# Relative attention on one NeuronCore: scores from zero-padded key copies, against scores on each head's own 32 rows

## What is computed

```python
Q, K, V = x @ W_q + b_q, x @ W_k + b_k, x @ W_v + b_v        # each to (B, 16 heads, 512, 8)
idx    = clip(k - q, -2, 2) + 2                              # 5 relative positions
scores = (einsum('bhqd,bhkd->bhqk', Q, K) + einsum('bhqd,qkd->bhqk', Q, rel_k_table[idx])) / sqrt(8)
attn   = softmax(where(causal, scores, -1e9), axis=-1)
out    = einsum('bhqk,bhkd->bhqd', attn, V) + einsum('bhqk,qkd->bhqd', attn, rel_v_table[idx])
y      = out.transpose(...).reshape(B, S, E) @ W_o + b_o
# then: x = x + y + six_windowed_layers(layernorm(x))
```

## Time and profile before

| | |
|---|---|
| time, three runs | 3923.24, 3927.83, 3929.47 us (median 3927.83) |
| profiled execution, its own time | 3928.65 us |
| its span | 3926.6 us |
| relative attention, start to last score work | about 0 to 563 us |
| windowed layers | the rest |
| PE busy over the whole span | 94% |
| DVE, ACT, POOL busy over the span | 78%, 58%, 66% |

### The profile page before, as it was taken

One profiled execution on the slowest core, in us unless ns is written; L12 is line 12 of the kernel. 1 busy time (PEld: TensorE's weight loads), 2 busy tenths in 40 slices (PEclk: granted clock), 3 DMA queues, 4 the chain that ended last, 5 costly groups with the idle time before them and its releaser, 6 DMA issues.

```text
span 3926.6 us, 163773 instructions
## 1 busy us (share of the span) xinstructions
PE 3690.6 (94%) x67712; PEld 2844.7 (72%) x67712; DVE 3058.0 (78%) x5829; ACT 2270.7 (58%) x4270; POOL 2597.4 (66%) x3029
## 2 busy tenths in 40 slices
PE   5999979999999999999999999999999999999998
PEld 3555557777767777677877678787677876777876
DVE  7666658888778888788887788887788887888876
ACT  3555546666546666456666366665466664566653
POOL 4545538787547887367887288775477873687870
PEclk8999989999999999999999999999999999999999
DMA  1000002222212222122222122222122221222220
GB/s 44 4 6 4 6 28 68 56 60 60 58 32 59 59 57 59 41 49 60 61 57 56 30 65 57 59 61 58 32 60 58 59 56 41 54 57 58 60 52 22
DMA packets 136313, 189.08 MB, mean 48 GB/s; under 512 B 38006, under 2 KB 58484, under 8 KB 135412
## 3 DMA queue, kind: packets, MB, share of 16 engines
q1 hardware_dynamic: 135540, 178.23, 17.7%
HBM read 22.67 MB, written 2.10 MB: 6 GB/s over the span
## 4 chain that ended last, share of the span: by engine, by line
PE 76%; issue 4%; DVE 2%; POOL 2%; ACT 0%; DMA 0%; POOLq 0%; SPq 0%; DVEq 0%; ACTq 0%
PE PS L1270 18%; PE PS L1417 10%; PE PS L1256 10%; PE PS L1294 8%; PE PS L1280 8%; PE PS L1258 8%; PE PS L1257 8%; PE PS L1476 2%; PE PS L1411 2%; PE PS L1454 1%; PE PS L1447 1%; POOL t L1182 1%; PE PS L1442 1%; POOL t L1187 0%; DVE m L1800 0%
## 5 line engine op out<-in xcount | busy, mean ns | idle before, releaser
L1182 POOL TENSOR_TENSOR t<-t 128x1024 f32<-128x1024 f32 x384 | 908.0, 2370 | 363.9 <-DVE t L1762 362.6
L1187 POOL TENSOR_TENSOR t<-t,rn 128x1024 f32<-128x1024 f32 x384 | 723.6, 1905 | 29.8 <-POOL rn L150 27.3
L1542 ACT ACTIVATE va<-PS 128x512 f32<-128x512 f32 x384 | 229.8, 599 | 614.4 <-PE PS L1258 611.6
L1760 DVE TENSOR_TENSOR t<-PS,rope 128x512 f32<-128x512 f32 x768 | 523.2, 681 | 26.1 <-ACT sq L1577 24.5
L1256 PE MATMUL PS<-w_hi,xh 128*128 128x512 f32 x1152 | 514.2, 446 | 22.3 <-DVE xl L1063 11.3
L1577 ACT ACTIVATE sq<-PS 128x512 f32<-128x512 f32 x768 | 454.1, 593 | 33.0 <-PE PS L1258 17.7
L1270 PE MATMUL PS<-constants,t 128*128 128x128 f32 x3072 | 443.8, 277 | 19.8 <-POOL t L1187 12.8
L1258 PE MATMUL PS<-w_lo,xh 128*128 128x512 f32 x1152 | 458.5, 398 | 0.0
L1257 PE MATMUL PS<-w_hi,xl 128*128 128x512 f32 x1152 | 457.5, 397 | 0.0
L1767 DVE TENSOR_REDUCE ss<-sq 128x16 f32<-128x1024 f32 x384 | 448.3, 1209 | 0.0
L1270 PEld LDWEIGHTS PS<-constants,t 128*128 128x128 f32 x3072 | 351.9, 141 | 68.9 <-POOL t L1187 15.9
(11 more groups left out here) (168 smaller groups left out, 7869.8 us busy)
## 6 DMA issues: line engine op xcount, KB each, us to landing
vs<-va SPq DMA_DIRECT2D x768, 130.0 KB
vs<-va SPq DMA_DIRECT2D x768, 65.0 KB
t<-in_L_ffn_Wqkv SPq DMA_DIRECT2D x18, 512.0 KB, 4.4
w_out<-in_L_ffn_Wo SPq DMA_DIRECT2D x6, 512.0 KB, 3.9
a_normed<-in_L_attn_x SPq DMA_DIRECT2D x8, 256.0 KB, 7.0
a_xo<-in_L_attn_x SPq DMA_DIRECT2D x8, 256.0 KB, 2.8
out<-total SPq DMA_DIRECT2D x8, 256.0 KB, 3.5
w_raw<-in_L_ffn_W SPq DMA_DIRECT2D x6, 341.0 KB
```

The source lines that it names most:

```text
L1182: pool.tensor_tensor(mine[:, i, :], mine[:, i, :], t2[:, i, :], ALU.add).then_inc(done, 1)
L1187: pool.tensor_tensor(h, h, bc(rn[:, H * i:H * (i + 1)], 2, HB), ALU.mult).then_inc(done, 1)
L1760: dve.tensor_tensor(o1, src, bc(rope[:, 2 * i, t, :], 1, 8), ALU.mult)
```

## The change

`kT` loses its four copies and has the same layout as `qT`. Each score product now reads only the 32 partitions of its head (`head(j, a)`), so PE works with tiles of 32 rows by 128 columns, and the two heads of a piece stand next to each other in PE's list, in different row tiles and different banks. The mask products stay as they are, over all 128 rows; the two of a piece now come first, and the scores of both heads after them.

A piece holds exactly two heads. So the fifth piece (four heads of 256 columns in a full slot) becomes two pieces that fill half of each bank: 6 pieces in place of 5. `maximum` and `weights` have one more instruction in a group, and the last two are half as long.

`join_keys` is one addition on 128 partitions. The memset of `kT` at the start of DVE's list is gone. `values(y, 0)` stands one piece later, and `values(y, 2)` moves from the end of group `y` to the place after `turned(y + 1, 0)`; the waits of `weights` on `val_mm` follow. GpSimd takes `join_queries` ahead of `keep_state` and `add_bias`, and `near_values` ahead of `add_bias`.

```diff
-        PIECES = 5
+        PIECES = 6
-        JOINS = 1 + G
+        JOINS = 2
-        kT = sb("a_kT", [P, NG, G, N], F32R)
+        kT = sb("a_kT", [P, NG, N], F32R)
...
             def join_keys(y):
                 wait_used(pool, ("proj", y, 1))
-                for r in range(G):
-                    rows = slice(32 * r, 32 * (r + 1))
-                    pool.wait_ge(joined, JOINS * y + 1 + r)
-                    pool.tensor_tensor(kT[rows, y % NG, r, 1:N], high[rows, 1, 0:N - 1].bitcast(F32), lowT[rows, 1, 0:N - 1],
-                                       ALU.add).then_inc(joined, 1)
-                pool.wait_ge(joined, JOINS * (y + 1))
+                pool.tensor_tensor(kT[:, y % NG, 1:N], high[:, 1, 0:N - 1].bitcast(F32), lowT[:, 1, 0:N - 1],
+                                   ALU.add).then_inc(joined, 1)
...
+            def head(j, a):
+                r = 2 * (j % 2) + a
+                return slice(32 * r, 32 * (r + 1))
...
             def natural(y, j):
...
-                q = lambda t: qT[:, g, P * t:P * (t + 1)]
-                k = lambda r, n: kT[:, g, r, 0:P * n]
+                blocks = (((3, 0, 4),), ((2, 0, 3), (0, 3, 1)), ((1, 0, 2),))[j // 2]
                 for a in range(2):
-                    b, r = bank(me, a), 2 * (j % 2) + a
-                    if j < 2:
-                        shut(b[:, 3 * P:4 * P], far_mask)
-                        done = score(b[:, 0:4 * P], q(3), k(r, 4))
-                    elif j < 4:
-                        shut(tiles_of(b, 2, 2), far_mask)
-                        score(b[:, 0:3 * P], q(2), k(r, 3))
-                        done = score(b[:, 3 * P:4 * P], q(0), k(r, 1))
-                    else:
-                        shut(every_second(b, 1), far_mask)
-                        for h in range(2):
-                            done = score(b[:, 2 * P * h:2 * P * (h + 1)], q(1), k(2 * a + h, 2))
+                    at, n = ((3, 1), (2, 2), (1, 1))[j // 2]
+                    shut(tiles_of(bank(me, a), at, n), far_mask)
+                for t, at, n in blocks:
+                    for a in range(2):
+                        rows = head(j, a)
+                        done = score(bank(me, a)[:, P * at:P * (at + n)], qT[rows, g, P * t:P * (t + 1)], kT[rows, g, 0:P * n])
                 done.then_inc(filled(me), 1)
...
             def turned(y, j):
...
+                    shut(tiles_of(bank(me, a), 0, (1, 2, 1)[j // 2]), far_mask_t)
+                for t, at in (((0, 0),), ((3, 0), (1, 1)), ((2, 0),))[j // 2]:
+                    for a in range(2):
+                        rows = head(j, a)
+                        done = score(bank(me, a)[:, P * at:P * (at - t) + N], kT[rows, g, P * t:P * (t + 1)],
+                                     qm[rows, y % 2, P * t:N])
...
                     turned(y, j)
+                    if j == 0 and y:
+                        values(y - 1, 2)
...
+                    if j == 3:
                         values(y, 0)
...
                 values(y, 3)
-                values(y, 2)
+            values(GROUPS - 1, 2)
...
-            dve.memset(kT[:].rearrange("p n g c -> p (n g c)").bitcast(F32), 0.0).then_inc(filled_in, 1)
             norm(0, TPS, 0)
```

More of the change, by code:

```diff
@@ L90, in constants @@
     row, query = np.arange(P)[:, None] % (2 * W), np.arange(P)[None, :]
+    c[:, C_FART:C_FART + P] = far.T
     c[:, C_SEL:C_SEL + P] = np.where(query < W, query == row, query % W + W == row)
-    c[:, C_FART:C_FART + P] = far.T
     c[0, C_NEAR:C_NEAR + H] = MASKED
@@ L365, in per_tile_head, with heads_of @@
             return h.rearrange("p t (h d) -> p t h d", h=H)
-        def of_heads(b, n):
-            return b[:, 0:G * n].rearrange("p (g c) -> p g c", g=G)
+        def heads_of(j, at, n):
+            return probs[:, 2 * (j % 2):2 * (j % 2) + 2, at:at + n]
         @block.sync
@@ L448, in _ @@
             keep_state(0)
-            pool.wait_ge(filled_in, 2 + G)
+            pool.wait_ge(filled_in, 2)
             join_queries(0)
@@ L457, in _ @@
                 s, p = divmod(y, NG)
+                if y + 3 < GROUPS:
+                    join_queries(y + 3)
                 if p == 1 and s + 1 < B:
@@ L460, in _ @@
                 if p == 3:
+                    near_values(s)
                     add_bias(s)
-                if y + 3 < GROUPS:
-                    join_queries(y + 3)
                 if p == 2 and s + 1 < B:
                     near_products(s + 1)
-                if p == 3:
-                    near_values(s)
                 if y + 3 < GROUPS:
@@ L505, in tiles_of @@
                 return b[:, P * at:P * (at + n)].rearrange("p (t c) -> p t c", t=n)
-            def every_second(b, at):
-                return b.rearrange("p (h t c) -> p h t c", h=2, t=2)[:, :, at, :]
+            def head(j, a):
+                r = 2 * (j % 2) + a
+                return slice(32 * r, 32 * (r + 1))
             def natural(y, j):
@@ L538, in turned @@
                 wait_slot(pe, me)
-                k = lambda r, t: kT[:, g, r, P * t:P * (t + 1)]
-                q = lambda t: qm[:, y % 2, P * t:N]
                 for a in range(2):
[L542 to L553, removed]
+                    shut(tiles_of(bank(me, a), 0, (1, 2, 1)[j // 2]), far_mask_t)
[4 more added lines that the diff above has]
+                                     qm[rows, y % 2, P * t:N])
                 done.then_inc(filled(me), 1)
@@ L557, in values @@
                 s, g = divmod(y, NG)
-                for j in ((0, 1), (2, 3), (4,), ())[kt]:
+                for j in ((0, 1), (2, 3), (4, 5), ())[kt]:
                     wait_used(pe, ("turn", y, j))
@@ L617, in _ @@
             pe.wait_ge(const_made, 3)
-            pe.wait_ge(filled_in, 2 + G)
+            pe.wait_ge(filled_in, 2)
             for j in range(PIECES):
@@ L680, in weights @@
                 wait_filled(act, me)
[L681 to L687, removed]
+                if y:
+                    act.wait_ge(val_mm, 4 * (y - 1) + (1, 3, 4)[j // 2])
+                at, n = ((0, 4), (4, 4), (8, 2))[j // 2]
+                act.activation(heads_of(j, P * at, P * n), bank(me)[:, :, 0:P * n], ACT.Exp, scale=SCALE_A).then_inc(used(me), 1)
             def copy_sums(y):
@@ L756, in maximum @@
                 else:
-                    target, source = maxima[:, y % 2, :, 5], bank(me).rearrange("p a (h c) -> p (a h) c", h=2)
+                    target, source = pair[:, :, 5], bank(me)[:, :, 0:2 * P]
                 dve.tensor_reduce(target, source, X, ALU.max).then_inc(used(me), 1)
@@ L841, in _ @@
             dve.wait_ge(const_in, 16)
+            dve.tensor_copy(kT[:, :, 0], rank["const"][:, C_SHUT:C_SHUT + 1].broadcast_to([P, NG])).then_inc(filled_in, 1)
             dve.wait_ge(filled_in, 2)
[L843 to L846, removed]
             dve.wait_ge(bias_made, 10)
```

## The result

The changed kernel takes 3986.77 us (median of 4 runs, 3982.11 to 3993.01), against 3925.53 for the kernel before (4 runs, 3922.84 to 3929.47): a ratio of 1.0152, 95% interval 1.0139 to 1.0165. The forecast was 3930, its range ended at 3960. The profiled execution after is the slowest of the four, 3993.01 us with a span of 3991.2.

The account below looks back on a forecast made before the run. PE was taken to bound relative attention. +17 us of PE work, -4 from relief of POOL and -11 at the start summed to +2 us on the profiled 3928.65, giving 3930 for the median, range 3900 to 3960.

Parts of the forecast that it names:

- the first reading: Relative attention after its start: PE is the bound, busy 470.30 of 492.00 us, at granted clock 0.99, the 2.4 GHz level.
- Pieces: Score pieces on PE: 512 columns 0.64 us, natural 384 and 128 0.76, turned 128 and 384 0.81, 256 columns 0.53.
- the change of shape: On PE, each switch between full-row mask products and 32-row score products costs 0.09 us.
- the exposed load: On PE, loading 128 fp32 weight columns is not hidden behind a switch of tile shape and costs 0.11 us.
- The sum at full clock: PE's work in relative attention grows by 0.54 us a group, or +17 us in 32 groups.
- POOL relief: Earlier near products and a shorter key join on POOL remove all of PE's wait for `qm`: -4 us.
- The start: Without the memset PE starts 5.5 us earlier; fewer joins save DVE's root steps 5.8 us; together -11 us, all on the path.
- Hidden loads: Rival, chance 0.10: PE takes score weight loads ahead while the masks run, saving 42 us: 3888.
- Loads in line: Rival, chance 0.08: fp32 loads of two row tiles go one after another, 0.11 more a piece, +42 us: 3972.
- The moved product missed: Rival, chance 0.17: without `values(y, 2)` there, PE waits 0.7 us for `qm` in the other 24 groups, +17: 3947.
- More relief: Rival, chance 0.15: with a quiet POOL the 1.29 us wait for maxima goes in seven sequences, -9, and more small waits: 3919.

## Why the prediction was wrong, step by step

**The step that failed** is the first reading: "at a granted clock of 0.99, so the 2.4 GHz level". I read it as a fixed condition of the stage, priced every new piece at it and never asked what the change does to it. No case and no rival had the clock in it. Measured: seven falls, together 119 us at 1.2 GHz. Six of them lie in the six sequences of the books. A full-clock sequence is 66.0 us (from the run with wider sums, which are in it with up to 0.2), so 6 x (66.0 - 63.64) = 14 us are the new form and 55.2 - 14 = **41 us the clock**. At the start 10.9 - 2.4 = 8.5 us of the lead go, up to 1.8 of them by the new form, so about 7 with the low clock. The two make 48 of the 56 us by which the stage missed its sum (+58.4 against +2).

**Pieces: right.** All four prices held within 0.01 us. The rows inside a piece fit the change of shape (0.09) and the exposed load (0.11) from which they were built, though these were read in the windowed layers, and the pair in two row tiles there has bf16 weights.

**The sum at full clock: nearly right in size.** Foretold +0.54 x 4 - 0.6 = +1.6 us a sequence, measured +2.4 (66.0 against 63.64). Both parts are off a little. PE is busy for 2.60 us more (63.50 against 60.90), foretold 2.16; 0.2 of that are the wider sums, the rest no run splits. And it waits for 0.24 us less (2.52 against 2.76), foretold 0.6: the waits for `qm` (0.7), for `neg` (0.5), for an output (0.2) and 0.2 at the maxima are gone, but 0.9 behind the moved `values(y, 0)` and 2 x 0.2 have come. I had asked which wait the move takes away and not which one it opens.

**POOL relief: right in size, the cause only in part.** The wait for `qm` fell from 4.3 to 0.4 us. The near products do begin sooner, which I named, but the short join is not needed for it: the kernel with full rows has the four joins and lost the wait too, and DVE's small instructions still stall (0.63 and 1.29 us) beside GpSimd.

**The start: mechanism right, worth wrong.** -10.9 us came at the first maxima, -11 foretold, but I said "It is all on the path; nothing else holds PE there". The low clock did: about 7 of the 8.5 us that were lost by the fourth group went with it, worked out from these two traces and not from a run of its own.

**The rivals.** Hidden loads: refuted, the pieces would be 0.11 shorter. Loads in line: refuted, by 0.18 for a pair and 0.65 a piece. The moved product missed: not for `qm` (0.4 us), but its sister `values(y, 0)` was, for 6.4 us. More relief: only 0.2 of the 1.29 went, and the small wait for `neg` (3.1 us in all).

**What stays open.** Why a fall comes in some sequences and not in others once the sums are wide, and why it then lasts up to 41 us, isn't settled; the runs of one kernel differ in it. That the seven regular falls need thin sums products and 32-row scores together is shown: taking away the first (wider sums) or the second (full rows throughout, or in the first group) leaves none or a few. The few that are left, in the fourth group, come with 32-row scores and no sums beside them, so the pair is not the only way to a fall. Which property of the work the chip weighs is not shown.

## What to carry to other kernels

Where a profile shows PE as the bound at the full clock, treat the clock as something that the change may move and not as a given: here it fell once in a sequence. Before putting products on fewer rows, look for the stretch in which they will stand beside other thin products, and price the case that it runs at 1.2 GHz. This rewrite saved PE no time at the full clock, so it had only that side to it. The cheapest test is to move the thin form into one group in four, or to widen the thin products, which cost next to nothing here (1.87 against 1.81 us for 16).

## What the runs showed that I had not expected

- The granted clock fell with PE 3.00 us busy in 3.00 us, and stayed at 1.2 GHz for 10 to 20 us of nearly unbroken work.
- Sixteen fp32 matmul instructions of 128 x 128 weights take 1.81 us with 36 columns and 1.87 with 108.
- Mask products twice, in bf16, did not hold the clock (0.92 from 70 to 560 us, 0.90 after), and the ratio rose from 1.0152 to 1.0203.
- 10.9 us won at the start of a stage, while the clock is low, were worth 2.4 us three groups later.
